# Transposes of x, context and the feed-forward x moved from TensorE to VectorE blocks and a round trip over DRAM

## The reference

```python
h = _ln(x, g1, be1)
x = _attn(h, h, Wq1, Wk1, Wv1, Wo1, bo1) + x          # 16 heads of 64
h = _ln(x, g2, be2)
x = _attn(h, context, Wq2, Wk2, Wv2, Wo2, bo2) + x
h = _ln(x, g3, be3)
y = h @ Wp + bp
a, gate = (y[..., :FF_HID], y[..., FF_HID:])          # FF_HID = 1024
x = a * jax.nn.gelu(gate, approximate=False) @ W2 + b2 + x
```

## Time and profile before

| | |
|---|---|
| median of 3 runs | 3034.53 us (3034.18 to 3035.11) |
| the profiled execution | 3032.93 us |
| its span, first to last instruction | 3031.1 us |
| mean granted TensorE clock | 0.995 |
| TensorE matmul busy | 2969.6 us, 98% |
| VectorE busy | 2296.2 us, 76% |
| ScalarE busy | 1883.4 us, 62% |
| GpSimd busy | 1424.5 us, 47% |
| self-attention, feed-forward | 96 to 1165 us, from 2468 us on |

### The profile page before, as it was taken

The page is one execution under the profiler, slowest core; times in us unless marked ns, Lnnn a source line. Parts: engine busy times, 40 slices in busy tenths (PEclk is TensorE's granted clock), DMA queues, the critical chain, the costliest instruction groups (busy, mean ns, idle before and its releaser), DMA issues. The chain is left out here.

```text
span 3031.1 us, 77419 instructions
## 1 busy us (share of the span) xinstructions
PE 2969.6 (98%) x25600; PEld 2591.1 (85%) x25600; DVE 2296.2 (76%) x3843; ACT 1883.4 (62%) x5618; POOL 1424.5 (47%) x976
## 2 busy tenths in 40 slices
PE   7999999999999999999999999999999979999999
PEld 6888888888888888788888888888888858888888
DVE  6777777777777777788888888888888855566554
ACT  6666666666666667677777777777777633223322
POOL 4555555555555555555555555555555530011000
PEclk9999999999999999999999999999999989999999
DMA  8788888888888888888888888888888830011000
GB/s 240 227 245 244 242 244 248 244 242 245 243 244 244 244 244 239 256 259 255 253 253 254 255 253 252 253 253 253 255 253 252 249 110 28 32 33 33 28 28 21
DMA packets 464444, 625.06 MB, mean 206 GB/s; under 512 B 57745, under 2 KB 397073, under 8 KB 464145
## 3 DMA queue, kind: packets, MB, share of 16 engines
q1 hardware_dynamic: 463024, 624.23, 69.1%
q10 hardware_dynamic: 1376, 0.27, 0.1%
HBM read 330.71 MB, written 293.60 MB: 206 GB/s over the span
## 5 line engine op out<-in xcount | busy, mean ns | idle before, releaser
L586 POOL TENSOR_TENSOR at_probs<-at_probs,at_row_inv 128x1024 f32<-128x1024 f32 x512 | 970.7, 1896 | 1057.8 <-DVE at_row_inv L792 1053.5
L637 ACT ACTIVATE at_probs<-at_ps_s,at_neg_max 128x256 f32<-128x256 f32 x2048 | 948.2, 474 | 143.0 <-DVE at_neg_max L765 94.3
L765 DVE TENSOR_REDUCE at_neg_max<-at_ps_s 128x2 f32<-128x512 f32 x1024 | 660.1, 683 | 193.6 <-PE at_ps_s L943 190.3
L784 DVE STREAM_TRANSPOSE at_blocks<-at_probs 128x1024 f32<-128x1024 f32 x512 | 630.9, 1232 | 2.7 <-POOL at_probs L586 2.0
L690 ACT ACTIVATE at_qk_hi<-at_ps_qk 128x512 fp32r<-128x512 f32 x512 | 305.9, 598 | 322.6 <-PE at_ps_s L943 182.5
L962 PE MATMUL at_ps_o<-at_probs_t,at_v 128*64 128x256 f32 x4096 | 500.3, 386 | 2.0 <-DMA at_probs_t<-at_turns 1.9
L875 PE MATMUL at_ps_qk<-at_h_hi,w_hi 128*128 128x256 f32 x1536 | 431.9, 304 | 11.3 <-ACT at_h_hi L660 4.9
L637 ACT ACTIVATION_READ_ACCUMULATOR at_probs<-at_ps_s,at_neg_max 128x1 f32 x2048 | 416.5, 203 | 0.0
L962 PEld LDWEIGHTS at_ps_o<-at_probs_t,at_v 128*64 128x64 f32 x4096 | 271.8, 137 | 148.9 <-issue 4.0
L875 PE MATMUL at_ps_qk<-at_h_hi,w_lo 128*128 128x256 f32 x1536 | 397.4, 281 | 0.0
L875 PEld LDWEIGHTS at_ps_qk<-at_h_hi,w_hi 128*128 128x128 f32 x1536 | 290.2, 189 | 123.0 <-issue 103.8
(11 more groups left out here) (108 smaller groups left out, 6617.3 us busy)
## 6 DMA issues: line engine op xcount, KB each, us to landing
at_turns<-at_blocks SPq DMA_DIRECT2D x2048, 128.0 KB, 2.5
at_probs_t<-at_turns SPq DMA_DIRECT2D x512, 512.0 KB, 4.4
at_xt<-in_x SPq DMA_DIRECT2D x32, 256.0 KB, 5.4
at_xres<-in_x SPq DMA_DIRECT2D x32, 256.0 KB, 3.3
after_self_attention<-at_yout SPq DMA_DIRECT2D x32, 256.0 KB, 2.6
at_xt<-after_self_attention SPq DMA_DIRECT2D x32, 256.0 KB, 5.6
at_xres<-after_self_attention SPq DMA_DIRECT2D x32, 256.0 KB, 3.6
after_cross_attention<-at_yout SPq DMA_DIRECT2D x32, 256.0 KB, 2.5
```

The lines of the kernel that those rows point to most:

```text
L586: pool.tensor_tensor(tile, tile, scale, ALU.mult).then_inc(probs_ready, 1)
L637: last = act.activation(probs[:, slot % 2, h, t], scores[:, slot % 2, h, t], ACT.Exp, bias=neg_max[:, slot % 2, i:i + 1], accum_out=row_su ...
L765: nc.vector.tensor_reduce(neg_max[:, slot, r], scores[:, slot, h], AX_X, ALU.max, negate=True).then_inc(neg_max_ready, 1)
L784: nc.vector.transpose(blocks[:, slot].rearrange("p (j a q) -> p a j q", j=QUADS, q=QUAD), probs[:, slot].rearrange("p h t (k j q) -> p (h ...
```

## The change

All transposes leave TensorE except the first in each of the two parts (sequence 0's h, and the feed-forward's group 0).

- Attention: GpSimd normalises in place in `xt`. VectorE transposes 32x32 blocks of the context in step 2 (`turn_context`) and of x in step 4 (`turn_x`) into `x_blocks`, SyncE stores them in four DMAs (`store_context`, `store_x`) behind the step's stores of probabilities, and loads them back two heads' pairs later (`load_context_back` in step 4, `load_x_back` in step 6) behind the loads of probabilities. `scale_shift` reads `x_back` in SBUF and stands in step 6. `high_context` becomes two instructions. `context_copy` is gone.
- Feed-forward: statistics in j = 1, normalisation and the block transpose (`turn`) in j = 2, four stores and a load on SyncE (`turn_back`), `scale_shift` from `x_back` in j = 6 directly ahead of the split. GpSimd waits for the attention's last store before its first residual.

The diff, cut to its core:

```diff
-TURN_CONTEXT, TURN_H = 2, 4
+TURN_CONTEXT, TURN_X = 2, 4
+X_TURN = TT * KT * QUAD
...
+    def turn(self, nc, dve, b):
+        dve.wait_ge(self.xnorm_ready, b + 1)
+        if counts(c := 16 * QUADS * (b - 1)):
+            dve.wait_ge(self.turn_stored, c)
+        nc.vector.transpose(self.blocks[:].rearrange("p (j a q) -> p a j q", j=QUADS, q=QUAD),
+                            self.xnorm[:].rearrange("p t (k j q) -> p (t k) j q", j=QUADS, q=QUAD)
+                            ).then_inc(self.turned, 1)
...
             def load_next(b, stage):
                 local = b - n * stage
-                sp.wait_ge(xnorm_ready, b)
+                if isinstance(b, int) and b == 1:
+                    sp.wait_ge(h_transposed, 1)
+                else:
+                    sp.wait_ge(x_turned, b - 1)
...
+            def store_bands(buffer, bands, stored):
+                for i in range(QUADS):
+                    sp.dma_start(bands[:, :, i].rearrange("j k n -> k j n"),
+                                 buffer[QUAD * i:QUAD * (i + 1)].rearrange("k (j n) -> k j n", j=QUADS)
+                                 ).then_inc(stored, 16)
+
+            def store_context(local):
+                sp.wait_ge(c_turned, local + 1)
+                store_bands(x_blocks, c_turns, c_turn_stored)
+
+            def store_x(b):
+                sp.wait_ge(x_turned, b)
+                store_bands(x_blocks, x_turns, x_turn_stored)
+
+            def load_context_back(local):
+                sp.wait_ge(c_turn_stored, 16 * QUADS * (local + 1))
+                sp.dma_start(c_t[:], c_turns.rearrange("j k i n -> (j k) (i n)")).then_inc(c_back_loaded, 16)
+
+            def load_x_back(b):
+                sp.wait_ge(x_turn_stored, 16 * QUADS * b)
+                sp.dma_start(x_back[:], x_turns.rearrange("j k i n -> (j k) (i n)")).then_inc(x_back_loaded, 16)
...
+                if context and p == TURN_CONTEXT + 2:
+                    load_context_back(b + 1 - n)
+                if ahead(part, stage) and p == TURN_X + 2:
+                    load_x_back(b + 1)
                 for pair in (p, p + 1):
                     if alive(part, pair, TURNED):
                         store_turn(b, pair)
+                if context and p == TURN_CONTEXT:
+                    store_context(b + 1 - n)
+                if ahead(part, stage) and p == TURN_X:
+                    store_x(b + 1)
...
             def scale_shift(b, stage):
-                act.wait_ge(h_transposed, b + 1)
-                if counts(c := b):
-                    act.wait_ge(h_ready, c)
+                first = isinstance(b, int) and b == 0
+                if first:
+                    act.wait_ge(h_transposed, 1)
+                else:
+                    act.wait_ge(x_back_loaded, 16 * b)
+                    act.wait_ge(h_ready, b)
...
-                act.activation(c_hi[:], c_t[:], ACT.Copy).then_inc(c_hi_ready, 1)
+                for k in range(KT):
+                    last = act.activation(tokens(c_hi[:, k]), by_token(c_t[:])[:, k], ACT.Copy)
+                last.then_inc(c_hi_ready, 1)
...
-                    if ahead(part, stage) and p == TURN_H:
+                    if ahead(part, stage) and p == 6:
                         scale_shift(b + 1, stage_ahead(part, stage))
-                    if ahead(part, stage) and p == 6:
                         high_h(b + 1)
...
+                if ahead(part, stage) and p == TURN_CONTEXT and stage_ahead(part, stage) == CROSS:
+                    turn_context(b + 1)
+                if ahead(part, stage) and p == TURN_X:
+                    turn_x(b + 1, stage_ahead(part, stage))
                 if alive(part, p + 1, NORMED):
                     inverse(b, p + 1)
...
-                if ahead(part, stage) and p == TURN_CONTEXT and stage_ahead(part, stage) == CROSS:
-                    transpose_context(b + 1)
-                if ahead(part, stage) and p == TURN_H:
-                    transpose_h(b + 1, stage_ahead(part, stage))
...
+            def turn_back(b):
+                sp.wait_ge(f.turned, b)
+                for i in range(QUADS):
+                    sp.dma_start(f.turns[:, :, i].rearrange("j k n -> k j n"),
+                                 f.blocks[QUAD * i:QUAD * (i + 1)].rearrange("k (j n) -> k j n", j=QUADS)
+                                 ).then_inc(f.turn_stored, 16)
+                sp.wait_ge(f.turn_stored, 16 * QUADS * b)
+                sp.dma_start(f.x_back[:], f.turns.rearrange("j k i n -> (j k) (i n)")).then_inc(f.back_loaded, 16)
...
                 if part in (FIRST, LOOP):
+                    if j == 1:
+                        f.norm_stats(nc, dve, b + 1, 1 - parity)
                     if j == 2:
-                        f.norm_stats(nc, dve, b + 1, 1 - parity)
-                    if j == 3:
                         f.norm_apply(nc, dve, b + 1, 1 - parity)
-                    if j == 5:
+                        f.turn(nc, dve, b + 1)
+                    if j == 6:
                         scale_shift(b + 1)
-                    if j == 6:
                         split_h(b + 1, 1 - parity)
...
-                if part in (FIRST, LOOP) and j == 4:
-                    transpose_h(b + 1)
```

125 lines of the change are left out of this document (71 added, 54 removed).

## The result

The changed kernel takes **3110.65 us** (median of 4 runs, 3107.72 to 3112.03) against 3034.36 for the kernel before (4 runs): a ratio of 1.0253, 95% interval 1.0238 to 1.0267. It is 76 us slower where 23.6 us less was forecast, and it lies outside the predicted range of 2986 to 3050. The profiled execution has a span of 3105.9 us (before: 3031.1).

A forecast was written before the change was run, and what follows sets the result against it. TensorE was taken as the bound, with VectorE binding around the turn of a cross sequence and DMA engines at 0.84. 50.2 - 41.6 + 15 = 23.6 us less than 3032.93 gives 3009.3, as a median 3011; range 2986 to 3050.

The forecast's parts named there:

- TensorE's gross gain: Attention: removing 95 groups of four transposes saves 41.8 us, and step 4's 0.27 excess another 8.4; gross 50.2 us.
- VectorE's block transposes at nothing: Attention: about 0.62 us each, 95 times, ahead of a reciprocal that waits for ScalarE anyway, so costed at nothing.
- Self stage at no cost: Self-attention: x lands some 5.5 us into step 6; about 0.3 us delay fits slack of about 0.8.
- Landing 6.1 into step 6 (cross): Cross stage: x's load back is issued about 2.1 us into step 6 and takes 4.0, landing at 6.1.
- the DMA engines' extra load: The added DMA traffic was given no price beyond the queue.
- no other store runs then: Cross step 6: argument that x's load would be faster than at_xt's 5.6 us, since no store runs beside it.
- What a late x costs: Each us of lateness costs the cross stage 32 us, and from a landing of 6.0 the self stage 31 more.
- Rival B: Slower: x comes back too late in step 6; a 5.1 us load gives +30 us, 3065; chance 0.19.
- ScalarE's term: Cross step 6: scale and shift ahead of at_qk_hi cost net 1.3 us a turn, 32 times, 41.6 us.
- a little delay would meet GpSimd's next instruction: Turn of a cross sequence: by the lock rule no delay of VectorE's at_c_hi is free; 0.6 us was counted won back.
- Feed-forward: Transposes and their wait save 1.33 us a group, the boundary gives back 0.35; 15 us for 15 groups (7 to 20).
- I am wrong if loads of probabilities come to bind TensorE.: Stated failure sign: TensorE's at_ps_o waiting for at_probs_t.

The follow-up runs named there:

- c_on_tensor: Changed kernel, but TensorE transposes the context again and VectorE copies it out of PSUM, without its stores and load; 3050.8 us, ratio 1.0056 to the kernel before.
- h_on_tensor_c_load_late: Changed kernel, but TensorE transposes cross's x again, the context's load follows step 4's eight stores, and feed-forward scale and shift move to j = 5; 2987.7 us.
- filled_gap: Changed kernel plus 18 matmuls that nobody reads at the end of each cross sequence's step 6, where TensorE idled; 3097.7 us.
- x_first_c_tensor: Changed kernel with x turned, stored and loaded back ahead of probabilities, context transposed by TensorE again, feed-forward scale and shift at j = 5; 3014.0 us.
- x_first_c_tensor_qk_first: x_first_c_tensor with ScalarE's step 6 order changed to scale and shift, at_qk_hi, at_h_hi, at_c_hi; 2992.0 us.
- both_on_tensor: Changed kernel, but in the cross stage TensorE transposes both x and the context as before; self stage and feed-forward stay changed; 3020.0 us.
- x_stale: Changed kernel with all transfers kept, but from sequence 2 on scale and shift reads columns loaded once, so ScalarE waits for no transfer; 3023.3 us.
- x_first: Changed kernel with x turned and stored ahead of step 4's second block of probabilities, and loaded back ahead of step 6's loads of probabilities; 3027.5 us.
- x_first_qk_first: x_first with ScalarE's step 6 order scale and shift, at_qk_hi, at_h_hi, at_c_hi, and feed-forward scale and shift at j = 5; 3018.7 us.

## Why the prediction was wrong

**TensorE's gross gain: right.** Steps 2 and 4 are 8.84 in the cross stage, step 4 of self 9.30. c_on_tensor confirms the split of step 4's excess too: with h off TensorE and the context on it, step 4 is 9.11, so 0.27 over 8.84 belongs to the context's copy; with the context off TensorE and h on it, step 4 is 9.28 (h_on_tensor_c_load_late), so the other 0.44 is h's transposes.

**VectorE's block transposes at nothing: right.** Steps 2 and 4, in which they stand, lost nothing.

**Self stage at no cost: right** in the loop (37.20 instead of 37.64; x lands 5.1 into step 6, ScalarE idle 0 in the median). The stage starts the cross stage only 7.5 us earlier instead of 13: the first two sequences, beside the loads of weights, took 5.0 us more (37.54 + 48.30 instead of 35.44 + 45.45).

**"Landing 6.1 into step 6 (cross)": the step that failed.** It was 8.07. Two of its parts were mis-sized: the load's issue (2.98, not 2.1) and its length (5.2, not 4.0). The text costed the queue by the issue times of x's own transfers and of the probabilities' and priced "the DMA engines' extra load" at nothing; the context's load in step 4, 256 KB on engines at 0.84, appears nowhere in it as something that x's stores and the loads of probabilities have to get past. c_on_tensor is the proof: without the context's trip x lands at 6.13 and the turn costs 1.31 where 1.3 was forecast. But the two terms behind that 6.1 were off even then, by amounts that cancel. The load took 4.7, not 4.0: it is issued 0.8 behind the second load of probabilities in the median, in both kernels, not the 1.7 to 2 that the 4.0 rested on. And it is issued at 1.45, not 2.1, since a store of x lands in 1.8, not 2.5. With the context's trip that store took 2.5 (the last of the four 2.8) and x's load 5.2. One reading of the rows was off too: the eight stores of step 4 end 1594.99 + 3.76 - 1591.45 = 7.30 into the step in the kernel before, and 7.32 with the change, not 6.8. The argument "no other store runs then" was wrong as well: SyncE issues eight stores of probabilities from 0.4 us after x's load on, so they run beside it.

**What a late x costs: linear in the prediction, steeper in fact.** Rival B had 1 us per us of lateness. Two more us gave 2.0 in step 6 (9.85 to 11.88) and, unforeseen, 0.84 in step 0 (9.85 to 10.69), because the granted clock fell after the wait. filled_gap shows that second part to be the clock's. In the means over the 30 sequences (11.93 and 10.53 against 9.91 and 9.95) it is 2.02 + 0.58 = 2.6 a turn, 81 us in 31 turns. The forecast had the cross stage 5.5 us longer (14.1 + 13.6 + 8.4 gained, 41.6 given back) and it was 93: of the 88 between them these are 81. Of the other 7, some 4 lie in the stage's first sequence (44.2 us, before 37.7), which lost 6.6 where the mean lost 2.9, and 3 in step 4, 8.94 in the mean over the 30 where 8.84 was forecast.

**ScalarE's term: right in sum, wrong in one part.** At a landing of 6.1 net 1.31 against 1.3. With x on the spot 0.7 against 0.37, because the 0.6 of at_c_hi comes back only when it starts after GpSimd's at_c_lo too. In x_first_c_tensor it starts at 1563.06 and takes 0.87; GpSimd's row is

```profile
1562.91 0.74 POOL L633 TENSOR_TENSOR at_c_lo<-at_c_t,at_c_hi 128x256 fp32r<-128x256 f32 x1
```

and ends at 1563.65. In the changed kernel, where at_c_hi starts at 1595.20 and GpSimd has nothing left, it takes 0.42. In x_first_c_tensor_qk_first it takes 1.18 and ends at 1559.83, GpSimd's at_h_lo beside it at 1559.55. In these two and in the kernel before it ends 0.27 to 0.28 after the GpSimd instruction that it overlaps. That is the reading the prediction took from the Trainium skill, page "SBUF — State Buffer", section "Who interferes with whom": the lock meets whichever GpSimd instruction runs then. The traces agree, and the prediction should have kept its own sentence ("a little delay would meet GpSimd's next instruction") in the sum.

**Feed-forward: right in mechanism, 15 forecast, 10.9 measured.** The transposes and their wait cost 1.27 in the median over the groups, not the 1.33 of the one read. The boundary gives back 0.55 a group, not 0.35, of which 0.44 is the late ff_h_lo. Scale and shift one step earlier (j = 5) removed it: step 7 is 4.21 in x_first_c_tensor.

**The rivals.** B named this failure and its place, and had 0.19. Its argument against itself, that x is issued 1.7 us behind the second load, fell: it was 0.8. It priced 5.1 us for the load at 3065, 19 of them in the self stage, which lost nothing; the load took 5.2 in the cross stage, but was issued 0.9 later and the clock fell, and so 3111. By the page "VectorE: DVE Perf Modes" of the Trainium skill, "Rules for kernel authors", the 128x128 transpose belongs on TensorE where a PSUM destination will do. For this change as it was made, the measurement agrees. But for one trip at a time it does not: x over VectorE and DRAM gave 2992.0, the context alone 2987.7, against 3020.0 with both on TensorE (the first two also have the feed-forward's j = 5, worth 6 to 8). Only the second is a plain comparison. The 2992.0 also has ScalarE's new order, which both_on_tensor was never given; with the old order it was 3014.0, and the 6 us between that and 3020.0 are no more than j = 5 gives.

**"I am wrong if loads of probabilities come to bind TensorE."** In the changed kernel they did not (9.0 us). As soon as x held nobody up they did: 27.7 (x_stale), 34.6 (x_first), 53.8 us (x_first_qk_first).

## What to carry to other kernels

When a change puts two new round trips into a queue whose engines are already at 0.84, cost each transfer by what the other new ones do to it, not by the nearest row of the old trace: here a 256 KB load that nobody waited for, and its four stores, made another one land nearly 2 us later, and undoing one of the two trips took 60 or 104 us off, although it gave TensorE its transposes back. Where a wait in the middle of the bounding engine's work is forecast to be some us long, look at what the granted clock did after the longest waits of the trace, and add it; look at many turns, since the same wait brought a fall at one and none at another. And ask of a late input what is queued behind its wait on the same engine, and in which order: moving one operation of ScalarE ahead of two others was worth 22 us.
